# One block of a causal convolution as an unsplit fp32 product, in a kernel of long convolutions and a linear layer with adapters

## The chip, the cores and the metric

The kernel runs on one core of one Trainium2 chip. The metric is the device time of one execution in microseconds, the median over the runs. A core has five engines that work side by side and meet only through semaphores: TensorE (PE, matmuls; its weight loads are shown apart as PEld), VectorE (DVE), ScalarE (ACT), GpSimd (POOL) and SyncE (SP, which here only issues DMAs).

## What is computed

`x` is (128, 32, 512): 128 rows `b`, 32 heads `h`, 512 positions. Two residual steps follow each other.

```
# step 1: a causal convolution of every head with its own filter of 512 lags
A = -exp(log_A_real) + 1j*A_imag ;  dtA = A * exp(log_dt)          # 64 modes a head
K[h, l] = 2 * Re( sum_n C*(exp(dtA)-1)/A * exp(dtA * l) )          # l = 0..511
y[b,h,t] = sum_{s<=t} K[h,t-s] * x[b,h,s]  +  D[h]*x[b,h,t]        # reference: by FFT
x = x + where(t < length[b], y, 0)
# step 2: a linear layer 512 -> 512 with a rank-16 adapter chosen per row b
x = x + x @ W.T + bias + (x @ A[id[b]].T) @ B[id[b]].T
```

All is float32.

## The kernel before

**Numbers.** A float32 matmul here is made of three in the type fp32r: each operand is split into a rounded part (hi) and a remainder (lo), and hi*hi, hi*lo and lo*hi are added in PSUM. Only the small products that make the filters take float32 operands as they are (L904, L906).

**Filters.** The 512 lags of a filter are written as 16 coarse times 32 fine steps, so that the filter of a head is a product of a 128x16 and a 128x32 matrix (two halves of 64 modes). Heads are made in four groups of eight (`GROUPS`). Per group, VectorE makes the phases (`turns`, `phases`, `whole`, `fraction`), ScalarE the sines (`group_sines`, L469), VectorE the factors (`multiply`, `scale`, L703 to L710), with magnitudes from ScalarE's exponential (`mags`), and TensorE the products (`group`, L904, into `k_ps`). ScalarE rounds the result (L480, L483), VectorE makes the remainder (`k_low`, L667), and ScalarE issues the store of the hi and lo parts, beside each other, to a table `k_pad` in HBM (`group_store`, L488). The table has 128 zeros in front of each filter.

**Strips.** A convolution is a product with a Toeplitz matrix. It is made by a DMA that reads `k_pad` at 128 starts, one position apart, one for each partition: `strip[p, j] = K[j + p - 127]` with j = 0..511, hi and lo interleaved, 4 KB a partition, 512 KB a head (L256, SP's queue). There are `SS = 6` strip buffers: the load of head h waits until head h-6 is convolved.

**A head on TensorE** (`head`, L923). x lies as four blocks of 128 positions by 128 rows. For m = 0..3, the lags of block m are the weights (`strip[.., m*P:(m+1)*P, t]`, 128x128) and the first 4 - m blocks of x are moved, so 512, 384, 256 and 128 columns, each three times: 12 matmuls into one of four PSUM banks.

**Around it.** ScalarE rounds x of a head (`split_x`, L458), VectorE makes its remainder (L738) and, four heads later, multiplies the convolved head by the mask of lengths into `z_all` (L744). In the loop over heads these come in a fixed written order: mask of head h-4, remainder of head h, then a step of a later group (`STEPS_AT`). Four buffers hold a split head (`XS`), so a split waits for the head four before. Where TensorE makes a group between heads stands in `K_AFTER`: group 1 after head 0, group 2 after head 7, group 3 after head 14. Fifteen idle matmuls (`keep_warm`) run before head 0.

**SP's queue** issues, in written order and each behind its waits: parameters, x in pairs of heads (pairs 0 to 6 before the strips, pair 7 on ScalarE's queue, later ones between strips at `X_AT`), strips, adapter tables and weights (`A_AT`, `B_AT`, `W_AT`), the first x tiles. A DMA behind a waiting one waits too.

**Tiles.** Step 2 works on 32 tiles of 4 rows b x 32 heads. The first two tiles are begun when 30 heads are masked (`part_of_x1` L848, `part_of_remainder` L851, L575), the last two heads are added afterwards. Then TensorE runs per tile 4 matmuls of the adapters (L948), 12 of the weights (L960) and 2 of the gathered B rows (L986, L987).

Of the kernel before, what the change touches and what calls it, by code (L numbers as in the profile page):

```python
# [22 lines left out]
PAD = P + L  # L23
# [36 lines left out]
SS = 6  # L60
ZS = 4
# [11 lines left out]
PRE = 7  # L73
X_AT = {7: 8, 9: 9, 12: 10, 14: 11, 16: 12, 18: 13, 20: 14, 22: 15}
IDS_AT = 6
A_AT, B_AT, W_AT = {10: 0, 13: 1}, {15: 0, 17: 1}, {24: 0, 26: 1}
# [4 lines left out]
K_AFTER = {1: 0, 2: 7, 3: 14}  # L81
WARM = 15
# [6 lines left out]
def build(nc, x_conv, x_tile, params, table, d_row, length, ids_all, w_t, bias, a_t, b_rows, out):  # L89
    ctx = ExitStack()  # L90
    with ctx:
# [9 lines left out]
        k_pad = nc.dram_tensor("k_pad", (NH, PAD, 2), F32, kind="Internal").ap()  # L101
# [31 lines left out]
        k_sb = sb("k_sb", [NA, KS, G, NC, 2])  # L133
        d_sb = sb("d_sb", [1, NH])
        row0 = sb("row0", [1, NA])
        zero = sb("zero", [2 * NH, P])
# [4 lines left out]
        strip = sb("strip", [P, SS, L, 2], F32R)  # L141
# [17 lines left out]
        h_b = sb("h_b", [BR, TS, 2 * P])  # L159
        h_s = sb("h_s", [BR, TS, 2 * P])  # L160
# [12 lines left out]
        def y_bank(s):  # L173
# [8 lines left out]
        x_landed = [sem(f"x_landed{n}") for n in range(NH // XP)]  # L182
        strip_landed = [sem(f"strip_landed{s}") for s in range(SS)]
# [10 lines left out]
        scaled, exponents, mags, turn_ready, angle_ready, cs_ready, phased = (  # L194
            sem(n) for n in ("scaled", "exponents", "mags", "turn_ready", "angle_ready", "cs_ready", "phased"))
# [31 lines left out]
        def _(sp):  # L227
# [8 lines left out]
            def store_table(e, part, done):  # L236
# [8 lines left out]
            sp.wait_ge(zeroed, 1)  # L245
            sp.dma_start(k_pad[:, 0:P, :].rearrange("h (o p) e -> h o (p e)", o=2),
                         zero[0:NH, :].unsqueeze(1).to_broadcast((NH, 2, P))).then_inc(pad_stored, 16)
            sp.dma_start(len_sb[:, :], length).then_inc(len_in, 16)
# [74 lines left out]
        def _(pool):  # L323
# [9 lines left out]
            g.memset(zero[:, :], 0.0).then_inc(zeroed, 1)  # L333
# [113 lines left out]
        def _(act):  # L447
# [23 lines left out]
            def group_store(k):  # L471
# [14 lines left out]
                if k >= 1:  # L486
                    act.wait_ge(k_stored, 16 * k)
                act.dma_start(k_pad[h0:h1, P:PAD, :].rearrange("h (a c) e -> a h (c e)", a=NA),  # L488
                              k_sb[:, s, 0:n, :, :].rearrange("a h c e -> a h (c e)")
                              ).then_inc(k_stored, 16)  # L490

            act.wait_ge(par_in, 16)
# [4 lines left out]
            for h in range(GROUPS[0][1]):  # L497
                act.activation(mag[:, h, :], tab[:, 0:NL], ACT.Exp, scale=zr[:, h:h + 1]).then_inc(mags, 1)
# [3 lines left out]
            split_x(0)  # L502
            split_x(1)
            group_store(0)
            act.dma_start(z_all[:, PRE * XP:(PRE + 1) * XP, :, :].rearrange("p h c b -> p h (c b)"),
                          x_conv[:, PRE * XP:(PRE + 1) * XP, :]).then_inc(x_landed[PRE], 16)
            group_sines(1)
            magnitudes(GROUPS[1][0], NH, 1)
            split_x(2)
            split_x(3)  # L510
            for h in range(XS, NH):
# [89 lines left out]
        def _(dve):  # L601
# [61 lines left out]
            def k_low(k):  # L663
# [4 lines left out]
                                k_hi[:, 0:n, :].bitcast(F32), ALU.subtract).then_inc(k_lo_done, 1)  # L668

            def group(k):  # L670
# [36 lines left out]
                def scale():  # L707
                    dve.wait_ge(mags, GROUPS[0][1] + min(k, 1))
# [153 lines left out]
            for t in range(EARLY_T):  # L862
                dve.wait_ge(xhi_early, t + 1)
                part_of_remainder(t, 0, EARLY, xlo_early)
# [4 lines left out]
            for t in range(EARLY_T):  # L869
                dve.wait_ge(xhi_done, t + 1)  # L870
                part_of_remainder(t, EARLY, NH, xlo_done)
# [18 lines left out]
        def _(pe):  # L890
# [6 lines left out]
            def group(k):  # L897
# [3 lines left out]
                if k >= KS:  # L901
                    pe.wait_ge(k_lo_done, k + 1 - KS)
# [175 lines left out]
```

## Time and profile before

| | us |
|---|---|
| median of 3 runs | 214.99 (214.13 to 215.07) |
| the profiled execution | 215.08 |
| its span, first to last instruction | 212.1 |
| TensorE busy | 191.1 (90%) |
| VectorE busy | 167.8 (79%) |
| ScalarE busy | 115.3 (54%) |
| strip loads, issue to landing, median of 31 | 8.7 |
| granted TensorE clock | 1.00 |

A matmul record lasts longer than the matmul keeps the array, because successive ones overlap. What a matmul costs in a stream is therefore the distance from one to the next; the chain of waits gives it as a stretch of time over a count. A record shows a float32 shape for fp32r operands of matmuls too.

### The profile page before, as it was taken

The page shows a single profiled execution, that of the slowest core. Times are in us where ns is not written, and L with a number is a line of the kernel's source. Part 1 is how long each engine was busy: PE and PEld are TensorE (multiplying, and loading weights), DVE is VectorE, ACT ScalarE, POOL GpSimd, SP SyncE. Part 2 cuts the span into 40 slices and gives each one's busy share as a digit, 9 for nine tenths or more (in the row PEclk, how much of TensorE's full clock was granted, in tenths as well). Part 3 has the DMA queues.
Part 4 walks back from the last instruction along what each step waited for, and adds up shares of the span by engine and source line. Part 5 has one row for each costly group of instructions (what it writes and reads, how often), then busy time and mean ns, then how long its engine had stood idle before and what let it go on. Part 6 is the DMA issues. An engine that isn't in the chain of part 4 may idle for free.

```text
span 212.1 us, 4365 instructions
## 1 busy us (share of the span) xinstructions
PE 191.1 (90%) x1061; PEld 166.4 (78%) x1061; DVE 167.8 (79%) x367; ACT 115.3 (54%) x331; POOL 89.7 (42%) x144
## 2 busy tenths in 40 slices
PE   0048899999989999889999999999999999999994
PEld 0045699999979899878888888888888888888883
DVE  3988388799699677777998888878787888878662
ACT  2747146434545346328667565666657565666530
POOL 4750000000565739256646454544546464554600
PEclk9999999999999999999999999999999999999999
DMA  5956999999999999965677666777767776665334
GB/s 149 357 232 172 350 406 272 417 415 406 411 410 410 407 409 412 403 209 188 203 246 223 211 217 202 240 199 216 225 198 219 216 214 211 226 202 175 121 99 148
DMA packets 21520, 56.46 MB, mean 266 GB/s; under 512 B 3266, under 2 KB 3970, under 8 KB 21250
## 3 DMA queue, kind: packets, MB, share of 16 engines
q1 hardware_dynamic: 18226, 47.25, 62.1%
q0 software_dynamic: 2560, 8.39, 13.4%
q10 hardware_dynamic: 720, 0.66, 1.2%
q8 instruction: 5, 0.08, 0.1%
q14 instruction: 9, 0.07, 0.1%
HBM read 45.64 MB, written 10.65 MB: 265 GB/s over the span
## 4 chain that ended last, share of the span: by engine, by line
PE 80%; DMA 10%; DVE 6%; POOL 1%; issue 1%; ACT 0%; SPq 0%; DVEq 0%; ACTq 0%
PE z_ps L923 24%; PE y_ps L960 19%; PE k_ps L960 19%; DMA strip<-k_pad 8%; PE z_ps L948 7%; PE y_ps L987 2%; PE y_ps L986 2%; PE k_ps L987 2%; PE k_ps L986 2%; DMA par<-params 1%; DMA k_pad<-k_sb 1%; PE k_ps L904 1%; PE y_ps L1009 1%; PE k_ps L1009 1%; PE y_ps L970 1%
## 5 line engine op out<-in xcount | busy, mean ns | idle before, releaser
L923 PE MATMUL z_ps<-xp,strip 128*128 128x512 f32 (+3 forms) x384 | 64.4, 327 | 3.0 <-DMA strip<-k_pad 3.0
L923 PEld LDWEIGHTS z_ps<-xp,strip 128*128 128x128 f32 x384 | 59.4, 196 | 8.0 <-DMA strip<-k_pad 4.2
L413 POOL DMA_INDIRECT b_hl<-b_tab,b_idx x32 | 38.3, 1198 | 15.9 <-issue 9.8
L960 PE MATMUL y_ps<-w_hi,xp 128*128 128x512 f32 x120 | 39.5, 390 | 0.0
L408 POOL CAST ag<-a_hl 128x128 fp32r x64 | 21.9, 343 | 41.6 <-PE z_ps L948 30.3
L960 PE MATMUL k_ps<-w_hi,xp 128*128 128x512 f32 x120 | 39.5, 390 | 0.0
L539 ACT ACTIVATE ag<-a_hl 128x64 fp32r x128 | 25.8, 249 | 21.0 <-issue 20.7
L458 ACT ACTIVATE xp<-z_all 128x512 fp32r<-128x512 f32 x32 | 19.8, 629 | 23.4 <-PE z_ps L923 21.7
L744 DVE TENSOR_TENSOR z_all<-z_ps,mask 128x512 f32<-128x512 f32 (+2 forms) x33 | 22.2, 672 | 9.1 <-PE z_ps L923 8.6
L738 DVE TENSOR_TENSOR xp<-z_all,xp 128x512 fp32r<-128x512 f32 x32 | 24.3, 764 | 5.0 <-ACT xp L458 4.7
L960 PEld LDWEIGHTS y_ps<-w_hi,xp 128*128 128x128 f32 x120 | 22.6, 188 | 4.3
L960 PEld LDWEIGHTS k_ps<-w_hi,xp 128*128 128x128 f32 x120 | 22.6, 188 | 4.2
L559 ACT ACTIVATE h_hi<-h_m 64x128 fp32r<-64x128 f32 x64 | 19.5, 305 | 7.5 <-DVE h_m L803 5.5
L960 PE MATMUL y_ps<-w_lo,xp 128*128 128x512 f32 x60 | 23.4, 390 | 0.0
L960 PE MATMUL k_ps<-w_lo,xp 128*128 128x512 f32 x60 | 23.4, 390 | 0.0
L395 POOL TENSOR_TENSOR a_hl<-a_raw,a_hl 128x512 fp32r<-128x512 f32 x4 | 6.3, 1592 | 39.5 <-ACT a_hl L529 39.5
L948 PEld LDWEIGHTS z_ps<-xp,ag 128*128 128x128 f32 x128 | 19.4, 188 | 2.9
L793 DVE TENSOR_TENSOR xp<-x_t,xp 128x512 fp32r<-128x512 f32 x30 | 20.3, 677 | 0.7 <-ACT xp L547 0.7
L789 DVE TENSOR_TENSOR x_t<-x_t,z_all 128x512 f32<-128x512 f32 x30 | 20.4, 680 | 0.5 <-DMA x_t<-x_tile 0.5
L547 ACT ACTIVATE xp<-x_t 128x512 fp32r<-128x512 f32 x30 | 19.0, 632 | 2.7 <-DVE x_t L789 2.1
L948 PE MATMUL z_ps<-xp,ag 128*128 128x256 f32 x128 | 20.1, 280 | 0.0
L552 ACT ACTIVATE h_b<-z_ps 64x256 f32<-64x256 f32 x32 | 12.1, 379 | 13.4 <-PE z_ps L948 13.3
(139 smaller groups left out, 232.4 us busy)
## 6 DMA issues: line engine op xcount, KB each, us to landing
strip<-k_pad SPq DMA_DIRECT2D x31, 512.0 KB, 8.7
x_t<-x_tile SPq DMA_DIRECT2D x32, 256.0 KB, 2.7
out<-a_raw SPq DMA_DIRECT2D x31, 256.0 KB, 2.5
z_all<-x_conv SPq DMA_DIRECT2D x15, 512.0 KB, 8.5
a_raw<-a_t SPq DMA_DIRECT2D x2, 512.0 KB, 9.0
x_t<-b_rows SPq DMA_DIRECT2D x2, 512.0 KB, 10.7
w_sb<-w_t SPq DMA_DIRECT2D x2, 512.0 KB, 10.4
b_tab<-b_hl SPq DMA_DIRECT2D x1, 1024.0 KB, 10.1
```

The source lines that it names most:

```text
L408: last = g.tensor_copy(ag[:, s, :, :, q, :].rearrange("p c e r -> p e c r"), src)
L413: g.indirect_dma_start(out=b_hl[:, t % BS, :].bitcast(F32), out_offset=None, in_=b_tab, in_offset=bass.IndirectOffsetOnAxis(ap=b_idx[:, t: ...
L458: act.activation(xp[:, h % XS, :, 0, :], z_all[:, h, :, :], ACT.Copy).then_inc(xc_hi_done, 1)
L539: last = act.activation(ag[:, s, :, e, q, :], src[:, e, :, :], ACT.Copy)
L559: act.activation(h_hi[o:o + BR, b, :], h_m[:, b, :], ACT.Copy).then_inc(hhi_done, 1)
L738: V.tensor_tensor(xp[:, h % XS, :, 1, :], z_all[:, h, :, :], xp[:, h % XS, :, 0, :].bitcast(F32), ALU.subtract).then_inc(xc_lo_done, 1)
L744: V.tensor_tensor(z_all[:, h, :, b0:b1], in_chunks(z_ps[:, h % ZS, :])[:, :, b0:b1], mask[:, :, b0:b1], ALU.mult).then_inc(z_masked, 1)
L789: V.tensor_tensor(xt, xt, z_rows(t), ALU.add).then_inc(x1_done, 1)
L793: V.tensor_tensor(xp[:, s % XS, :, 1, :], in_chunks(x_t[:, s % XT, :]), xp[:, s % XS, :, 0, :].bitcast(F32), ALU.subtract).then_inc(xlo_do ...
L923: last = nc.tensor.matmul(z_ps[:, h % ZS, m * P:L], strip[:, h % SS, m * P:(m + 1) * P, t], xp[:, h % XS, 0:LC - m, e, :], start=(n == 0), ...
L948: last = nc.tensor.matmul(h_ps[:, s % TS, 0:2 * P], ag[:, s % TS, c, :, :, :].rearrange("p e b r -> p (e b r)"), xp[:, s % XS, c, :, :].re ...
L960: last = nc.tensor.matmul(y_bank(s), xp[:, s % XS, c, e, :], w[:, c, :], start=(n == 0), stop=False)
```

## The change

The block of the longest lags (m = 3, lags of 384 and more against the first 128 positions of x) is no longer three fp32r products. It is one product of unsplit float32 numbers: the lags from a new table `k_one` in HBM, without hi and lo, in which four heads are interleaved, and x as it was loaded. The strips keep 384 lags (3 KB a partition). A block `far` holds the far lags of four heads, 2 KB a partition, 256 KB a DMA, in three buffers. Each group therefore has two stores and each four heads one more load. The far weights of one head lie four words apart.

With it come moves in the written orders: group 1 is made ahead of head 0; its magnitudes, and the later ones, are single ScalarE activations placed between the splits in place of one VectorE product and one exponential over 24 heads; the padding and length DMAs go to ScalarE's queue and x pair 7 to SP's; some loads move by a head or so; and at the handover to the tiles VectorE makes the remainder of tile 1 after head 31's first mask instead of before it.

```
-PAD = P + L
+LM = L - P            # 384
+NQ = 4 ; ONE = 2 * P ; QS = 3
-PRE = 7
-X_AT = {7: 8, 9: 9, 12: 10, 14: 11, 16: 12, 18: 13, 20: 14, 22: 15}
-IDS_AT = 6 ; A_AT, B_AT, W_AT = {10: 0, 13: 1}, {15: 0, 17: 1}, {24: 0, 26: 1}
-SPLIT_B = {22: 0, 23: 1, 24: 2, 25: 3}
-K_AFTER = {1: 0, 2: 7, 3: 14} ; WARM = 15
+PRE = 8
+X_AT = {7: 8, 10: 9, 13: 10, 15: 11, 18: 12, 20: 13, 22: 14, 24: 15}
+IDS_AT = 5 ; A_AT, B_AT, W_AT = {9: 0, 12: 1}, {17: 0, 19: 1}, {24: 0, 26: 1}
+SPLIT_B = {23: 0, 24: 1, 25: 2, 26: 3}
+K_AFTER = {2: 7, 3: 14} ; WARM_0, WARM_1 = 15, 2
+MAGS_AT = {4: (24, 28), 5: (28, 32)}
...
# SP's queue
+            def load_last(q):
+                sp.wait_ge(last_stored, 16 * (q * NQ // G + 1))
+                src = bass.AP(tensor=k_one.tensor, offset=k_one.offset + NQ * (q * ONE + 1), ap=[[NQ, P], [1, P * NQ]])
+                sp.dma_start(far[:, q % QS, :, :].rearrange("p l x -> p (l x)"), src).then_inc(last_landed[q % QS], 16)
                 if h == 0:
                     load_strip(h, 0, 0, L // 2, strip_begun)
-                    load_strip(h, 0, L // 2, L, strip_landed[0])
+                    load_strip(h, 0, L // 2, LM, strip_landed[0])
+                    load_last(0)
                 else:
-                    load_strip(h, h % SS, 0, L, strip_landed[h % SS])
+                    if h > 0 and h % G == 0:
+                        load_last(h // NQ)
+                    load_strip(h, h % SS, 0, LM, strip_landed[h % SS])
+                if h % G == 2:
+                    load_last(h // NQ + 1)
...
# ScalarE: group_store, after the store to k_pad (group 0's copy is made by VectorE in k_low)
+                if k:
+                    act.wait_ge(last_stored, 16 * k)
+                    act.activation(k_last[...], k_ps[0:NA, s, 0:n * NC]..., ACT.Copy).then_inc(k_last_put, 1)
+                act.wait_ge(k_last_put, k + 1)
+                act.dma_start(k_one[h0 // NQ:h1 // NQ, :, :]..., k_last[NA // 2:NA, ...]).then_inc(last_stored, 16)
...
# ScalarE: order before the loop over heads
             group_sines(0)
             split_x(0)
+            magnitudes(*GROUPS[1])
+            group_store(0)
+            group_sines(1)
             split_x(1)
-            group_store(0)
-            act.dma_start(... x pair 7 ...)
-            group_sines(1)
-            magnitudes(GROUPS[1][0], NH, 1)
+            magnitudes(16, 18)
+            group_store(1)
             split_x(2)
+            magnitudes(18, 24)
             split_x(3)
...
# VectorE: start, and handover to the tiles
             fraction()
-            exponents_of(GROUPS[1][0], NH)
             remainder(0)
-            remainder(1)
             multiply()
             scale()
+            remainder(1)
+            k_low(1)
+            masks()
             remainder(2)
             remainder(3)
-            masks()
...
             part_of_x1(0, 0, EARLY, x1_early)
-            head(NH - 2)
             part_of_x1(1, 0, EARLY, x1_early)
-            both part_of_remainder(t, 0, EARLY, xlo_early)
+            head(NH - 2)
+            part_of_remainder(0, 0, EARLY, xlo_early)
             head(NH - 1, 0, EARLY_T * BT)
             part_of_x1(t, EARLY, NH, x1_done) for both tiles
-            part_of_remainder(t, EARLY, NH, xlo_done) for both tiles
+            part_of_remainder(0, EARLY, NH, xlo_done)
+            part_of_remainder(1, 0, EARLY, xlo_early)
+            part_of_remainder(1, EARLY, NH, xlo_done)
...
# TensorE
-                terms = [(m, t, e) for m in range(LC) for t, e in ((0, 0), (0, 1), (1, 0))]
+                terms = [(m, t, e) for m in range(LC - 1) for t, e in ((0, 0), (0, 1), (1, 0))]
                 ... the products of terms, as before ...
+                q = h // NQ
+                if h % NQ == 0:
+                    pe.wait_ge(last_landed[q % QS], 16 * (q // QS + 1))
+                nc.tensor.matmul(z_ps[:, h % ZS, LM:L], far[:, q % QS, :, h % NQ], z_all[:, h, 0, :],
+                                 start=False, stop=True).then_inc(conv_done, 1)
...
             group(0)
             pe.wait_ge(xc_hi_done, 1)
-            keep_warm(WARM)
+            keep_warm(WARM_0)
+            group(1)
+            keep_warm(WARM_1)
```

## Rows read from the trace of the kernel before

**Rows 1.** The page: busy time, share and count of TensorE.
```profile
PE 191.1 (90%) x1061; PEld 166.4 (78%) x1061; DVE 167.8 (79%) x367; ACT 115.3 (54%) x331; POOL 89.7 (42%) x144
```

**Rows 2.** The chain in order of time: start us, us, what.
```profile
25.33 13.85 PE z_ps L923 x84
39.17 0.57 PE k_ps L904 x16
...
60.48 11.17 DMA strip<-k_pad
71.70 15.90 PE z_ps L923 x96
87.62 0.69 DVE z_all L744
...
95.00 2.77 PE y_ps L960 x12
...
98.24 0.47 PE z_ps L948 x4
```

**Rows 3.** Timeline, VectorE, 80 to 84 us: start, busy, what [idle before].
```profile
81.74 0.69 DVE L744 TENSOR_TENSOR z_all<-z_ps,mask 128x512 f32<-128x512 f32 x1 [0.37 <-PE z_ps L923]
...
83.70 0.69 DVE L744 TENSOR_TENSOR z_all<-z_ps,mask 128x512 f32<-128x512 f32 x1 [0.19 <-PE z_ps L923]
```

**Rows 4.** Groups by form, TensorE: the unsplit products (busy, mean ns).
```profile
L904 PE MATMUL k_ps<-ee,gg 128*16 128x32 f32 x64 | 2.9, 205 | 13.5 <-DVE ee L710 13.5
```

**Rows 5.** Timeline, TensorE, around groups 1 and 3.
```profile
24.55 0.64 PE L904 MATMUL k_ps<-ee,gg 128*16 128x32 f32 x16
...
25.12 0.20 PE L906 MATMUL k_ps<-d_sb,row 1*16 1x8 f32 x2
...
25.26 5.06 PE L923 MATMUL z_ps<-xp,strip 128*128 128x512 f32 x28
...
53.84 0.46 PE L904 MATMUL k_ps<-ee,gg 128*16 128x32 f32 x10
```

**Rows 6.** Groups by form, weight loads: strided strip, contiguous x, 16 columns.
```profile
L923 PEld LDWEIGHTS z_ps<-xp,strip 128*128 128x128 f32 x384 | 59.4, 196 | 8.0 <-DMA strip<-k_pad 4.2
L960 PEld LDWEIGHTS k_ps<-w_hi,xp 128*128 128x128 f32 x120 | 22.6, 188 | 4.2
...
L904 PEld LDWEIGHTS k_ps<-ee,gg 128*16 128x16 f32 x64 | 2.4, 104 | 13.7 <-issue 13.4
```

**Rows 7.** Stretches: engines' busy time, granted clock, DMA share, GB/s at the end.
```profile
50.00:60.00 10.00, 10.00 (x76) 9.32 (x75) 8.30 (x15) 5.84 (x11) 4.60 (x4) 1.00 1.03 409
```

**Rows 8.** DMA issues: the stores of filters, KB each, us to landing.
```profile
k_pad<-k_sb ACTq DMA_DIRECT2D x4, 32.0 KB, 5.5
```

**Rows 9.** The strip loads' line (L256), all of them.
```profile
DMA to landing us min/median/max: 4.0/8.5/11.6
```

**Rows 10.** Waits: engine, line, for whom, us in total, times, longest.
```profile
PE z_ps L923 <- DMA strip<-k_pad: 3.0, 5, 1.3
...
SPq L256 <- DMA k_pad<-k_sb: 3.3, 2, 2.3
```

**Rows 11.** Timeline of the start, 6 to 38 us, ScalarE and VectorE.
```profile
6.44 1.89 ACT L498 ACTIVATE mag<-tab,zr 128x48 f32<-128x48 f32 x8
...
14.67 0.37 ACT L480 ACTIVATE k_hi<-k_ps 16x256 fp32r<-16x256 f32 x1 [2.72 <-PE k_ps L906]
...
17.27 1.28 ACT L463 ACT_TABLE_LOAD   x1
...
27.35 0.69 DVE L738 TENSOR_TENSOR xp<-z_all,xp 128x512 fp32r<-128x512 f32 x1 [1.17 <-ACT xp L458]
...
37.84 0.42 DVE L710 TENSOR_TENSOR ee<-work,mag 128x256 f32<-128x256 f32 x1
```

**Rows 12.** Timeline of the handover to the tiles, VectorE.
```profile
88.79 1.41 DVE L851 TENSOR_TENSOR xp<-x_t,xp 128x480 fp32r<-128x480 f32 x2
...
90.12 0.18 DVE L744 TENSOR_TENSOR z_all<-z_ps,mask 128x32 f32<-128x32 f32 x1
```

More of the change, by code:

```diff
@@ L22 @@
 BR = BT * R
-PAD = P + L
+LM = L - P
+NQ = 4
+ONE = 2 * P
 assert NA * NC == L and 2 * NS == P and 2 * BR == P
@@ L60 @@
 SS = 6
+QS = 3
 ZS = 4
@@ L99, in sem @@
             return ctx.enter_context(nc.semaphore(name))
-        k_pad = nc.dram_tensor("k_pad", (NH, PAD, 2), F32, kind="Internal").ap()
+        k_pad = nc.dram_tensor("k_pad", (NH, P + LM, 2), F32, kind="Internal").ap()
+        k_one = nc.dram_tensor("k_one", (NH // NQ, ONE, NQ), F32, kind="Internal").ap()
         b_tab = nc.dram_tensor("b_tab", (2 * AD * R, L), F32, kind="Internal").ap()
@@ L140, in build @@
         pos = mask[:, :, :].bitcast(I32)
-        strip = sb("strip", [P, SS, L, 2], F32R)
+        strip = sb("strip", [P, SS, LM, 2], F32R)
+        far = sb("far", [P, QS, P, NQ])
         xp = sb("xp", [P, XS, LC, 2, P], F32R)
@@ L159, in build @@
         h_b = sb("h_b", [BR, TS, 2 * P])
+        zero = h_b[:, 0, 0:P]
         h_s = sb("h_s", [BR, TS, 2 * P])
@@ L182, in build @@
         x_landed = [sem(f"x_landed{n}") for n in range(NH // XP)]
+        last_landed = [sem(f"last_landed{s}") for s in range(QS)]
+        last_stored, k_last_put = sem("last_stored"), sem("k_last_put")
         strip_landed = [sem(f"strip_landed{s}") for s in range(SS)]
@@ L193, in build @@
             sem(n) for n in ("ea_ready", "zr_ready", "th_ready", "rc_ready", "rec_ready", "ez_ready"))
-        scaled, exponents, mags, turn_ready, angle_ready, cs_ready, phased = (
-            sem(n) for n in ("scaled", "exponents", "mags", "turn_ready", "angle_ready", "cs_ready", "phased"))
+        scaled, mags, turn_ready, angle_ready, cs_ready, phased = (
+            sem(n) for n in ("scaled", "mags", "turn_ready", "angle_ready", "cs_ready", "phased"))
         k_hi_put = sem("k_hi_put")
@@ L496, in _, with magnitudes @@
             act.wait_ge(table_in, 16)
-            for h in range(GROUPS[0][1]):
-                act.activation(mag[:, h, :], tab[:, 0:NL], ACT.Exp, scale=zr[:, h:h + 1]).then_inc(mags, 1)
+            def magnitudes(h0, h1):
+                for h in range(h0, h1):
+                    act.activation(mag[:, h, :], tab[:, 0:NL], ACT.Exp, scale=zr[:, h:h + 1]).then_inc(mags, 1)
+            magnitudes(*GROUPS[0])
             act.wait_ge(angle_ready, 1)
@@ L519, in _ @@
                         group_sines(k)
+                if h in MAGS_AT:
+                    magnitudes(*MAGS_AT[h])
                 if h in SPLIT_B:
@@ L858, in _ @@
             part_of_x1(0, 0, EARLY, x1_early)
-            head(NH - 2)
             dve.wait_ge(xt_landed[1], 16)
             part_of_x1(1, 0, EARLY, x1_early)
-            for t in range(EARLY_T):
-                dve.wait_ge(xhi_early, t + 1)
-                part_of_remainder(t, 0, EARLY, xlo_early)
+            head(NH - 2)
+            dve.wait_ge(xhi_early, 1)
+            part_of_remainder(0, 0, EARLY, xlo_early)
             head(NH - 1, 0, EARLY_T * BT)
@@ L868, in _ @@
                 part_of_x1(t, EARLY, NH, x1_done)
-            for t in range(EARLY_T):
-                dve.wait_ge(xhi_done, t + 1)
-                part_of_remainder(t, EARLY, NH, xlo_done)
+            dve.wait_ge(xhi_done, 1)
+            part_of_remainder(0, EARLY, NH, xlo_done)
+            dve.wait_ge(xhi_early, 2)
+            part_of_remainder(1, 0, EARLY, xlo_early)
+            dve.wait_ge(xhi_done, 2)
+            part_of_remainder(1, EARLY, NH, xlo_done)
             head(NH - 1, EARLY_T * BT, NB)
@@ L902, in group @@
                     pe.wait_ge(k_lo_done, k + 1 - KS)
+                    pe.wait_ge(k_last_put, k + 1 - KS)
                 for i in range(h1 - h0):
@@ L922, in head @@
                         pe.wait_ge(strip_landed[0], 16)
-                    last = nc.tensor.matmul(z_ps[:, h % ZS, m * P:L], strip[:, h % SS, m * P:(m + 1) * P, t],
-                                            xp[:, h % XS, 0:LC - m, e, :], start=(n == 0), stop=(n == len(terms) - 1))
-                last.then_inc(conv_done, 1)
+                    nc.tensor.matmul(z_ps[:, h % ZS, m * P:L], strip[:, h % SS, m * P:(m + 1) * P, t],
+                                     xp[:, h % XS, 0:LC - m, e, :], start=(n == 0), stop=False)
+                q = h // NQ
[3 more added lines that the diff above has]
+                                 start=False, stop=True).then_inc(conv_done, 1)
             pe.wait_ge(d_in, 16)
```

46 lines of the change are left out of this document (23 added, 23 removed).

## The prediction

> **What bounds the kernel now.** I read the page first: TensorE is busy 90% of the span [rows 1]. Then the chain in order of time [rows 2]. It has three parts: a start until about 25 us (parameters, filter of the first eight heads, stored and read back as strips), 32 convolution heads until 87.62 + 1.96 = 89.6, and 32 tiles to the end. In the tiles the chain never leaves TensorE, and the change touches nothing there: that part stays.
>
> In the convolution part the chain is almost all TensorE: 84 matmuls (7 heads) in 13.85 us, and one step of 11.17 us on the strip loads, from 60.48 on. Undisturbed, a head takes 83.70 - 81.74 = 1.96 us [rows 3]. Beside it the DMA engines are full (share 1.03, 409 GB/s) [rows 7]. TensorE stood 3.0 us for strips in 5 waits, 1.3 for the very first [rows 10]. What the later ones cost is read from the chain: head 15 begins at 39.88 + 13.85 + 0.71 = 54.4, head 23 at 71.70, 17.3 us for 8 heads that need 15.7: 1.6 lost. So two resources lie close together here. A cheaper head is worth its full price only where the strips keep up.
>
> **A head.** Removed: three matmuls of 128 columns. Added: one product of unsplit fp32, 128 x 128 x 128. Prices of the nine that stay: 512 columns 2.77 / 12 = 0.23 us, 256 columns 0.47 / 4 = 0.118 [rows 2], 384 columns between them, 0.174. 3 x (0.23 + 0.174 + 0.118) = 1.57. The three narrow ones and the uncovered first weight load of the next head therefore cost 1.96 - 1.57 = 0.39.
>
> The fp32 product is not in the trace at this size. L904 is the nearest: 64 matmul records for 32 products [rows 4], so an unsplit product is two loads and two matmuls. Ten of them end 0.46 us after the first begins, and one lasts 0.19 or 0.20 (mean 205 ns, the slower first group included): (0.46 - 0.19) / 9 = 0.030 us apart for 32 columns [rows 5]. Four times the columns give 4 x 0.030 = 0.12 each, 0.24 for the two, and a matmul of 0.12 covers the next load of 128 columns about exactly (a 256-column one does so at 0.118). Bounds: below, each pass at half of that, 0.12 for the pair and some 0.06 of load left uncovered; above, either of the first two rivals. I take 0.24, and 0.02 to 0.03 because the strip's loads are slower than L960's (196 against 188 ns [rows 6]): 1.57 + 0.24 + 0.02 = 1.83. **A head saves 0.13 us.**
>
> The rate is the same as four passes of 128 columns at 2.4 GHz, 0.21 us. The Trainium skill (FP8 and Floating Point Precision, TensorE Precision Notes) says that true fp32 takes four passes; by it alone the pair is 0.21 and the head 1.80. The trace's 0.24 stands in the sum.
>
> **The start.** Group 1's 18 matmuls (25.26 - 24.55 = 0.71 us [rows 5]) move from behind head 0 to ahead of it. Their cover there is the wait for the first strip. Group 1's factors come about as early as before: the deferred exponents (1.3 us of VectorE) are gone, but ScalarE now issues a second store and loads the sine table (1.28, as the exponential one [rows 11]) before the sines. The eight magnitudes of group 1 (1.89 us for eight) and their table fit, to a few tenths, into ScalarE's wait of 2.72 us before the first k_hi and the split that moves away from there [rows 11]. Ahead of strip 1's end the queue holds 256 + 128 KB of strip 0, 256 KB of the far block and 384 KB: 1024 KB as now (256 + 256 + 512). It gains only what pair 7, moved from ScalarE's queue to the front, took away, 512 KB or 1.28 us at most; I take 0.9. Head 1 starts at about 24.4 instead of 25.26, and group 1 is no longer between. Moving the padding and lengths to ScalarE's queue costs 0.8 us there, before parameters at 2.9 us that it waits for anyway: nothing.
>
> This gain does not all reach head 8. In heads 4 to 9 VectorE runs nearly without a gap: remainder 4 begins at 27.35, after ScalarE [rows 11], and group 2's scaling ends at 37.84 + 0.42 = 38.26. After the change ScalarE has 16 single magnitudes (0.24 each) and a further table load among splits 2 to 5, so remainder 4 starts no earlier (I get 27.2), and the factors of group 2 are again there at 38.25. TensorE would end head 7 at 24.4 + 7 x 1.83 = 37.2 and waits 1.0 us. Head 8 then starts at 39.0 instead of 39.88 (39.17 and 0.71 of group 2 [rows 2]): **-0.8**. If ScalarE were not late, it would be up to -1.8.
>
> **Heads 8 to 31.** 7 heads, group 3 as now, 17 heads: 24 x 0.13 = **-3.1**, as long as strips land.
>
> **The strips.** A head loads 384 KB, and 64 KB as its share of a far block, instead of 512 KB: at 409 GB/s 1.12 us instead of 1.28, 12.5% less, where the head on TensorE gets 7% shorter. Against it stands SP's queue, which now waits for two stores of a group, the second about 0.9 us behind the first on ScalarE's queue (copy 0.45, issue 0.36); a store lands 5.5 us after its issue [rows 8], and SP waits for it already now (3.3 us in 2 waits [rows 10]). What is queued behind that wait is every later strip and x pair, six heads ahead of TensorE. For head 16: group 2 done at 39.0, its three copies behind masks and splits 2.1, the second store 0.9 more, 5.5 to land: 47.5, with the queue then nearly run dry, and the first landing 4.0 later at the least [rows 9]. From 51.5 to strip 25 stand 10 strips (0.96), 3 far blocks (0.64) and 7 other loads (1.28), 20.5 us, the first of them landed: 71.4, where TensorE wants head 25 at 39.0 + 7 x 1.83 + 0.8 + 10 x 1.83 = 70.9. So half a microsecond is lost there and some at heads 19 to 21; bounds 0 and 2.7 more than now. I leave the present 1.6: **0**.
>
> **The handover to the tiles.** Now head 31's mask, due at 89.6, waits for two remainders (88.79 to 90.2) and runs at 90.12 [rows 12]. The change puts only one before it: **-0.5**. The second is 0.7 us and is due only for tile 1, some 3.5 us after the first matmul. The table stores and x_tile loads follow the strips by the same order and come earlier with them.
>
> **Sum:** -0.8 - 3.1 - 0.5 = -4.4. The profiled execution took 215.08 (span 212.1 and 3.0 around it), the median is 214.99: 215.1 - 4.4 = **210.7**.
>
> **Rivals.**
>
> *A break at each change of number type (0.18).* The pipeline empties where the matmul's kind changes. [Rows 5] show it: 16 matmuls 0.030 apart should take 0.48, but L906 begins 0.57 after the first, 0.09 late, and the convolution's first is also late by 0.08; then the next load of 128 columns (0.11) is uncovered. These changes are of shape, one of them without a change of type, which speaks against; all changes of type are also changes of shape, so nothing excludes it. The change makes two per head: 2 x (0.09 + 0.11) = 0.40, a head of 2.23, +0.27 x 31 = 8.4. The strips then are never late (-1.6), the start gives -0.9, the handover -0.5: +5.4, **220.5**. It decides once the two breaks cost more than 0.13 a head.
>
> *Weights four words apart (0.12).* The far block has four heads interleaved, so its weights are read at every 16th byte. Two words apart already costs 196 against 188 ns [rows 6]. If a load takes double, 0.236, it is no longer covered: 0.236 + 0.236 + 0.12 after eight matmuls of 1.47 is 2.07, +0.11 x 31 = 3.4, less the same 3.0: **215.5**, no change. The Trainium skill (SBUF — State Buffer, Door 1: The DMA port swizzle) says that reads need two hits in each 16-byte line for full bandwidth, which the strip has and the far block has not, though the same passage calls a stride of 4 fp32 free. No row here reads weights so.
>
> *The queue (0.10).* The mechanism is right but the second store and the far blocks make SP late at heads 8, 16 and 24, and the engines restart slowly after running dry. The strips then give back 2.7: **213.3**.
>
> **Chances.** My forecast has 0.60, with a range of its own of 208.6 to 212.5 (the DMA waits gone and half a microsecond elsewhere, or 1.8 more waits); with the queue 0.10, the strided load 0.12, the break 0.18. The range for all is 208.6 to 216.2, which leaves out the break. Half a percent, 1.1 us, is what a measurement here can tell from none: faster holds the first case and most of the queue, 0.67; same, the rest and half of the strided load, 0.13; slower 0.20.
>
> **What would show it.** The masks of late heads 1.83 us apart; two loads and two matmuls of about 0.12 for the far block, the next head's load close behind; a wait of TensorE for the scaling of group 2 of about 1 us; head 8 at 39.0; the last head done near 85.5; head 31's first mask right after it. Wrong would be: masks 2.07 or 2.2 apart, gaps around the far matmuls, TensorE standing for far blocks, or a table load that delays split 2 and with it head 2.

## The result, and the profile after

The changed kernel takes **213.34 us** (median of 4 runs, 213.16 to 213.79), the kernel before 215.00 (4 runs): a ratio of 0.9935, 95% interval 0.9906 to 0.9965. It is faster by 0.7%, where 210.7 us (2.0%) was forecast. The profiled executions differ by 215.08 - 213.79 = 1.29 us, and only 0.4 of that is span (212.1 to 211.7). The rest is time around the span, 3.0 and 2.1 us. The profiled execution of the kernel after is the slowest of its four; the others have spans of 211.1 to 211.3.

The page of the kernel after, its engines line (it answers to [rows 1]):

```profile
PE 193.8 (92%) x1031; PEld 169.6 (80%) x1031; DVE 167.6 (79%) x367; ACT 123.0 (58%) x359; POOL 90.3 (43%) x144
```

Thirty matmuls fewer (1061 to 1031), and yet TensorE is busy 2.7 us longer. The groups by form say which instruction is dear (busy us, mean ns of one | idle before). First the matmuls of the convolution, then weight loads; L955 is the strip (L923 before), L960 the far block, L998 the tiles (L960 before), L936 the unsplit products of the filters:

```profile
L955 PE MATMUL z_ps<-xp,strip 128*128 128x512 f32 x96 | 30.2, 422 | 0.3 <-DMA strip<-k_pad 0.3
...
L960 PE MATMUL z_ps<-z_all,far 128*128 128x128 f32 x64 | 20.0, 394 | 0.3 <-DMA far<-k_one 0.3
```
```profile
L955 PEld LDWEIGHTS z_ps<-xp,strip 128*128 128x128 f32 x288 | 49.7, 197 | 4.1 <-DMA strip<-k_pad 0.5
L998 PEld LDWEIGHTS k_ps<-w_hi,xp 128*128 128x128 f32 x120 | 22.5, 188 | 4.2
...
L960 PEld LDWEIGHTS z_ps<-z_all,far 128*128 128x128 f32 x64 | 17.5, 322 | 0.5 <-DMA far<-k_one 0.5
```

64 records for 32 products: an unsplit product is two loads and two matmuls here too. A load of the far block lasts 322 ns, against 197 for one whose weights are two words apart and 188 for words side by side [rows 6]. The waits for strips have gone from 3.0 us to 0.3. The timeline of three heads in the middle, matmuls and then loads (start, busy, what; the last row of each is cut by the end of the window), answers to [rows 3]:

```profile
67.04 1.83 PE L955 MATMUL z_ps<-xp,strip 128*128 128x512 f32 x9
68.70 0.62 PE L960 MATMUL z_ps<-z_all,far 128*128 128x128 f32 x2
69.08 1.83 PE L955 MATMUL z_ps<-xp,strip 128*128 128x512 f32 x9
70.74 0.62 PE L960 MATMUL z_ps<-z_all,far 128*128 128x128 f32 x2
71.12 1.12 PE L955 MATMUL z_ps<-xp,strip 128*128 128x512 f32 x4
```
```profile
68.58 0.55 PEld L960 LDWEIGHTS z_ps<-z_all,far 128*128 128x128 f32 x2
69.03 1.02 PEld L955 LDWEIGHTS z_ps<-xp,strip 128*128 128x128 f32 x5
```

A head is 69.08 - 67.04 = 2.04 us, where 1.83 was forecast and 1.96 was there before. Two far loads take from 68.58 to 69.03, when the next head's load begins: 0.45 us for two, with matmuls of 0.12 to cover them. That is where the gain of the head went, as e1 to e4 and e7 show below.

The start and the handover, TensorE and VectorE (they answer to [rows 5] and [rows 12]):

```profile
24.40 1.85 PE L955 MATMUL z_ps<-xp,strip 128*128 128x512 f32 x9 [0.27 <-DMA strip<-k_pad]
...
87.44 1.83 PE L955 MATMUL z_ps<-xp,strip 128*128 128x512 f32 x9
...
90.69 1.17 PE L1008 MATMUL y_ps<-w_hi,xp 128*128 128x512 f32 x4 [0.97 <-ACT xp L606]
```
```profile
88.33 0.65 DVE L880 TENSOR_TENSOR xp<-x_t,xp 128x480 fp32r<-128x480 f32 x1
89.76 0.19 DVE L773 TENSOR_TENSOR z_all<-z_ps,mask 128x32 f32<-128x32 f32 x1 [0.78 <-PE z_ps L960]
```

| start on TensorE, us | before | after | difference |
|---|---|---|---|
| head 1 | 25.26 | 24.40 | -0.86 |
| head 8 | 39.81 | 39.59 | -0.22 |
| head 15 | 54.35 | 54.76 | +0.41 |
| head 23 | 71.70 | 71.12 | -0.58 |
| head 31 | 87.42 | 87.44 | +0.02 |
| first tile | 91.05 | 90.69 | -0.36 |

The account of the profiled executions closes. Head 1 gains 0.86. Seven heads at +0.08 and 23 more at +0.08 give back 2.4. The 1.6 us of waits for late strips, read from the chain as lost between heads 15 and 23, are gone. The handover gives 0.37. Together -0.4, the difference of the spans.

### The profile page after: what moved, and what is told of

It is laid out like the page before. It is cut to its first block, busy times and chain, and to the rows that moved or that the text cites. A ratio compares the mean times of both kernels' runs of the same rounds, so it can differ in the third digit from the quotient of the medians.

```text
span 211.7 us, 4345 instructions
## 1 busy us (share of the span) xinstructions
PE 193.8 (92%) x1031; PEld 169.6 (80%) x1031; DVE 167.6 (79%) x367; ACT 123.0 (58%) x359; POOL 90.3 (43%) x144
## 4 chain that ended last, share of the span: by engine, by line
PE 87%; DVE 5%; DMA 4%; POOL 1%; issue 1%; SPq 1%; ACT 0%; DVEq 0%; ACTq 0%
PE z_ps L955 23%; PE y_ps L998 19%; PE k_ps L998 19%; PE z_ps L986 7%; PE z_ps L960 7%; DMA strip<-k_pad 3%; PE y_ps L1025 2%; PE y_ps L1024 2%; PE k_ps L1025 2%; PE k_ps L1024 2%; DMA par<-params 1%; DMA k_pad<-k_sb 1%; PE y_ps L1047 1%; PE k_ps L1047 1%; PE y_ps L1008 1%
## 5 line engine op out<-in xcount | busy, mean ns | idle before, releaser
L955 PE MATMUL z_ps<-xp,strip 128*128 128x512 f32 (+2 forms) x288 | 58.4, 347 | 0.3 <-DMA strip<-k_pad 0.3
L955 PEld LDWEIGHTS z_ps<-xp,strip 128*128 128x128 f32 x288 | 49.7, 197 | 4.1 <-DMA strip<-k_pad 0.5
L424 POOL CAST ag<-a_hl 128x128 fp32r x64 | 23.3, 368 | 43.1 <-PE z_ps L986 29.5
L998 PE MATMUL k_ps<-w_hi,xp 128*128 128x512 f32 x120 | 39.5, 390 | 0.0
L998 PE MATMUL y_ps<-w_hi,xp 128*128 128x512 f32 x120 | 39.5, 390 | 0.0
L767 DVE TENSOR_TENSOR xp<-z_all,xp 128x512 fp32r<-128x512 f32 x32 | 25.8, 807 | 8.2 <-ACT xp L474 8.1
L998 PEld LDWEIGHTS k_ps<-w_hi,xp 128*128 128x128 f32 x120 | 22.5, 188 | 4.2
L998 PEld LDWEIGHTS y_ps<-w_hi,xp 128*128 128x128 f32 x120 | 22.5, 188 | 4.2
L998 PE MATMUL y_ps<-w_lo,xp 128*128 128x512 f32 x60 | 23.4, 390 | 0.0
L998 PE MATMUL k_ps<-w_lo,xp 128*128 128x512 f32 x60 | 23.4, 390 | 0.0
L960 PE MATMUL z_ps<-z_all,far 128*128 128x128 f32 x64 | 20.0, 394 | 0.3 <-DMA far<-k_one 0.3
```

What stands on the lines that cost most here:

```text
L424: last = g.tensor_copy(ag[:, s, :, :, q, :].rearrange("p c e r -> p e c r"), src)
L767: V.tensor_tensor(xp[:, h % XS, :, 1, :], z_all[:, h, :, :], xp[:, h % XS, :, 0, :].bitcast(F32), ALU.subtract).then_inc(xc_lo_done, 1)
L955: nc.tensor.matmul(z_ps[:, h % ZS, m * P:L], strip[:, h % SS, m * P:(m + 1) * P, t], xp[:, h % XS, 0:LC - m, e, :], start=(n == 0), stop=F ...
L960: nc.tensor.matmul(z_ps[:, h % ZS, LM:L], far[:, q % QS, :, h % NQ], z_all[:, h, 0, :], start=False, stop=True).then_inc(conv_done, 1)
L998: last = nc.tensor.matmul(y_bank(s), xp[:, s % XS, c, e, :], w[:, c, :], start=(n == 0), stop=False)
```

## The experiments

All are variants of the changed kernel, except e8, which is the kernel before with one order altered; e5, e6, e9 and e10 alter two or more things, as said at each. "Head" is the distance of two heads' first matmuls where nothing waits. Times are medians, and the span is that of the profiled execution. The kernel before ran beside each group and took 213.88 us in one group and 214.96 in another, so runs of different groups are compared by their ratios, not by their times.

| run | us | before beside it | ratio, 95% interval | span | far load, ns | head, us |
|---|---|---|---|---|---|---|
| after | 213.34 | 215.00 | 0.9935 (0.9906 to 0.9965) | 211.7 | 322 | 2.04 |
| e1_contig | 211.23 | 214.96 | 0.9835 (0.9757 to 0.9913) | 208.6 | 191 | 1.79, 1.83 |
| e2_pairs | 212.70 (one) | 214.96 | | 210.6 | 196 | 1.80, 1.83 |
| e3_rounded4 | 212.22 (one) | 214.96 | | 210.1 | 313 | 1.81 |
| e4_rounded1 | 214.18 (one) | 214.96 | | 212.1 | 192 | 1.70 |
| e5_contig_ids | 211.48 | 213.88 | 0.9876 (0.9835 to 0.9917) | 208.9 | | |
| e6_pairs_ids | 210.83 | 213.88 | 0.9837 (0.9794 to 0.9880) | 209.0 | 196 | 1.80, 1.83 |
| e7_strides | 212.12 (one) | 213.88 | | 210.0 | 186 to 330 | 1.79 to 2.04 |
| e8_handover | 213.71 (one) | 213.88 | | 211.6 | | |
| e9_spread | 211.58 | 214.91 | 0.9858 (0.9824 to 0.9891) | 209.3 | 196 | 1.80, 1.83 |
| e10_spread_order | 211.85 | 214.91 | 0.9864 (0.9833 to 0.9894) | 209.8 | 196 | 1.80, 1.83 |

**e1_contig: the same product, its weights side by side.** The far block is stored and loaded head by head instead of four heads interleaved; the same bytes, in rows of 512 B instead of 2 KB, and the same number of DMAs and matmuls. The source address of the load and the copies before the stores follow the new order and are left out here.

```diff
+IL = 1
+IN = NQ // IL
-k_one = nc.dram_tensor("k_one", (NH // NQ, ONE, NQ), ...)
+k_one = nc.dram_tensor("k_one", (NH // IL, ONE, IL), ...)
-far = sb("far", [P, QS, P, NQ])
+far = sb("far", [P, QS, IN, P, IL])
...
-nc.tensor.matmul(z_ps[...], far[:, q % QS, :, h % NQ], z_all[:, h, 0, :],
+nc.tensor.matmul(z_ps[...], far[:, q % QS, h % NQ // IL, :, h % IL], z_all[:, h, 0, :],
```

> The changed kernel with the far lags of each head by themselves (in the table k_one, in the stores and in the block far), so that the far weights are read contiguously; the bytes are the same, in rows of 512 B instead of 2 KB. Theory 1, the stride: a load at every 16th byte takes twice as long, so here the two far loads last about 190 ns in the profile instead of 322, the head goes from 2.04 to 1.83 us and the waits that I predicted appear (group 2's factors, about 1 us, and some strips): 210.5 to 212. Theory 2, the number type: a load of 128 columns of unsplit fp32 takes 0.22 us however it lies: loads 322 ns, heads 2.04, 213.3. Theory 3, a break at each change of type: also 2.04 and 213.3, with loads that start late.

**e2_pairs: weights two words apart**, as the strip's are (`IL = 2`).

> The changed kernel with the far lags of two heads interleaved instead of four: weights two words apart, as in the strips. Theory 1 with a 16-byte line as the limit: as with contiguous weights, loads near 196 ns and heads of 1.83 us, total within 0.5 us of that run. Theory 1 with a cost that grows with the stride: loads near 250 ns, heads of 1.9. Theories 2 and 3: 2.04 and 213.3.

Far loads of e1 and e2, and the timeline of a late head of e1:

```profile
L963 PEld LDWEIGHTS z_ps<-z_all,far x64: 187/191/192, 23.1 to 86.2; 128*128 128x128 f32 x64
```
```profile
L963 PEld LDWEIGHTS z_ps<-z_all,far x64: 194/196/331, 23.0 to 88.2; 128*128 128x128 f32 x64
```
```profile
78.99 1.86 PE L958 MATMUL z_ps<-xp,strip 128*128 128x512 f32 x9
80.68 0.39 PE L963 MATMUL z_ps<-z_all,far 128*128 128x128 f32 x2
80.82 1.86 PE L958 MATMUL z_ps<-xp,strip 128*128 128x512 f32 x9
```

With side-by-side weights the load is 191 ns and the head 80.82 - 78.99 = 1.83 us (1.79 in heads 1 to 7), where 1.83 was forecast. So the pair of unsplit fp32 matmuls was priced about right, the break at each change of number type that the first rival charged with 0.40 us a head is not there (it would have stayed), and the whole 0.21 us by which the head missed is the distance of the weights. Two words apart (e2) are as good as one. The time fell to 211.23, by 2.1 us, not by 31 x 0.21 = 6.5: the first tile starts 3.15 us earlier than in the kernel after (87.54). What eats the other 3.4 is the second question. e2 had e1's head and only 212.70, in one execution.

**e3_rounded4 and e4_rounded1: is it the number type?** The far product is one rounded (fp32r) product of x's high part instead of the unsplit one; the low part's share is left out. Weights four words apart in e3 and side by side in e4:

```diff
-far = sb("far", [P, QS, P, NQ])
+far = sb("far", [P, QS, IN, P, IL], F32R)          # IL = 4 in e3, 1 in e4
-... z_all[:, h, 0, :],
+... xp[:, h % XS, 0, 0, :],
```

> The changed kernel with the far block taken as fp32r and multiplied with the rounded part of x alone: one load and one matmul instead of two and two (it leaves out the remainder of x and part of the lags' precision in the far block). The weights lie four words apart as in the change. Theory 1: this load lasts about 322 ns too, though its type is fp32r, and the head is about 1.90 us (1.47 for eight matmuls, 0.12, 0.22 for the load, 0.12 for the next head's). Theory 2 and 3: the load lasts 197 ns and the head takes 1.57 + 0.06 + 0.06 + 0.06 = 1.75.

> The same single fp32r product with the far weights contiguous (it leaves out the same parts). Theories 1, 2 and 3 all expect a load of 188 ns and a head of about 1.75 us on TensorE, where strips allow it; beside the run with four words it shows what the stride alone costs in type fp32r. The time is then set by the strips: 209 to 211.

Far loads of e3, then e4:

```profile
L963 PEld LDWEIGHTS z_ps<-xp,far x32: 309/313/313, 22.9 to 87.7; 128*128 128x128 f32 x32
```
```profile
L963 PEld LDWEIGHTS z_ps<-xp,far x32: 186/192/331, 23.1 to 88.4; 128*128 128x128 f32 x32
```

The load costs the same 313 ns in fp32r: the price is that of the distance, not of the number type. A single dear load costs the head 1.81 - 1.70 = 0.11 us, a pair 0.24 (2.04 - 1.80): each load beyond its cover by about 0.12. And e4, with one product in fp32r, has a head 0.10 us below e2's with a pair in unsplit fp32: one more matmul of 128 columns and nothing for a change of type.

e4 missed its 209 to 211 us. The shortest head of all, 1.70, has the longest span of the variants, 212.1. Its waits are longer, and two of its heads run at half the clock. Stretches of e4 (engines' busy time, granted clock, DMA share, GB/s), and its timeline there:

```profile
60.00:64.00 4.00, 3.74 (x22) 3.21 (x20) 3.90 (x6) 2.19 (x4) 3.48 (x3) 1.00 1.05 414
64.00:68.00 4.00, 0.84 (x2) 0.78 (x3) 3.93 (x7) 1.15 (x2) 1.83 (x2) 0.79 1.05 377
68.00:72.00 4.00, 4.00 (x14) 3.52 (x14) 3.94 (x7) 1.15 (x2) 0.19 (x1) 0.50 1.02 399
```
```profile
67.16 3.22 PE L958 MATMUL z_ps<-xp,strip 128*128 128x512 f32 x9 [3.24 <-DVE xp L770]
...
70.28 3.10 PE L958 MATMUL z_ps<-xp,strip 128*128 128x512 f32 x9
```

TensorE stood 3.24 us for VectorE and then ran two heads at 0.50 of the clock, 1.2 GHz, 3.1 and 3.0 us instead of 1.70. e2 stood 3.24 us as well and ran one head slowly, 3.3 us. In e1 the wait at this place was 1.74, and the clock stayed at 1.00. But e3 stood longest, 3.28 us at the same place, and its clock stayed at 1.00 too (its timeline and its stretch of the wait):

```profile
68.01 1.83 PE L958 MATMUL z_ps<-xp,strip 128*128 128x512 f32 x9 [3.28 <-DVE xp L770]
```
```profile
64.00:68.00 4.00, 0.73 (x6) 0.61 (x5) 3.90 (x7) 1.31 (x3) 2.58 (x2) 1.00 1.04 401
```

So a wait of this length does not by itself bring the slow stretch, and what decides stays open. The slow head is 1.5 us of the 2.0 by which the profiled executions of e1 (210.67) and e2 (212.70) differ. Each variant has one profiled execution; one of e1's four runs, 212.72 us at a mean clock of 0.992, resembles e2, and two runs of the kernel before beside them, 217.06 and 215.95 us, show a mean clock of 0.984.

**What the wait is.** VectorE of e1 (start, busy, what), then its TensorE:

```profile
60.94 1.32 DVE L751 CAST id_f<-ids 128x160 f32<-128x160 int32 x1
62.30 0.25 DVE L752 TENSOR_SCALAR id_f<-id_f 128x160 f32<-128x160 f32 x1
...
63.50 1.17 DVE L757 TENSOR_SCALAR b_idx<-ids,tab 128x32 int32<-128x32 int32 x1
...
66.38 1.17 DVE L770 TENSOR_TENSOR xp<-z_all,xp 128x512 fp32r<-128x512 f32 x1
```
```profile
65.96 1.82 PE L958 MATMUL z_ps<-xp,strip 128*128 128x512 f32 x9 [1.74 <-DVE xp L770]
```

In step 20 of its loop VectorE computes the adapter numbers for the tiles, which select each row's adapter, in six instructions, from 60.94 to 64.67. A head leaves VectorE 0.46 us beside its mask and remainder (1.83 - 0.69 - 0.68), so it is late for head 21, by 2.0 us with the restart. The kernel after does the same work (61.83 to 64.6) and TensorE does not wait: there a head leaves 0.67 us and VectorE has more lead.

**e5_contig_ids and e6_pairs_ids: the six instructions in step 16 instead of 20**, with the far weights of e1 (`IL = 1`) and of e2 (`IL = 2`).

```diff
-                if h == 20:
+                if h == 16:
                     adapter_ids()
```

> Contiguous far weights, and the adapter ids (six VectorE instructions) made in the loop's step 16 instead of 20. In the run with contiguous weights TensorE stood about 2 us before head 21, where VectorE was busy with the ids from 60.9 to 64.7, two of them at 1.2 to 1.3 us instead of 0.25 while GpSimd worked. Theory A (VectorE late with remainder 21): the wait goes, about 1 us of strip waits takes its place (strip 21 landed at 65.34, where head 21 would start at 64.3), 209.3 to 210.5. Theory B (the strips are the limit in any case): no gain, 211.2.

> The same with the far lags of two heads interleaved (rows of 1 KB instead of 512 B; the loads had measured the same 196 ns). Theory A: the 3.5 us wait before head 21 and the stretch at half clock behind it both go, 209 to 210; if the larger rows help the strips, up to 0.5 us below the contiguous one. Theory B: 212.5.

The wait is gone from head 21 and stands elsewhere. ScalarE of e6, and the strips' waits of e6 (engine, what <- releaser: us in total, times, longest):

```profile
57.26 0.30 ACTq L502 DMA_DIRECT2D k_pad<-k_sb  x1
57.60 0.40 ACT L507 ACTIVATE k_last<-k_ps 16x256 f32<-16x256 f32 x1 [4.13 <-DVE k_sb L695]
...
58.40 0.63 ACT L477 ACTIVATE xp<-z_all 128x512 fp32r<-128x512 f32 x1 [0.40 <-PE z_ps L963]
```
```profile
PE z_ps L958 <- DMA strip<-k_pad: 1.2, 2, 0.9
```

Group 3's low half is now late on VectorE (56.78), ScalarE waits for it 4.13 us with the splits of two heads queued behind, head 18 starts 1.7 us late, and the strips of heads 25 and 27, behind group 3's stores, are late by 1.2 in all. It is the queue behind a waiting instruction that the prediction feared, for another reason. Both theories missed: e6 forecast 209 to 210 and e5 209.3 to 210.5, against 210.83 and 211.48. e6 has the lowest time of all, but before beside it was low as well: its ratio, 0.9837, is e1's 0.9835. That the move gained anything over e1 is not shown. Over e2 it is likely, as the wait of 3.24 us and the slow head are gone.

**e7_strides: distances of one to four words in one kernel.** The far weights of heads 0 to 7, 8 to 15, 16 to 23 and 24 to 31 are read 1, 2, 3 and 4 words apart; except for heads 0 and 4 the words read are not the head's own, so its far product is another. How the block is stored and loaded is the same for all heads.

```diff
+... far[...].rearrange("p i l x -> p (i l x)")[:, 0:(h // 8 + 1) * (P - 1) + 1:h // 8 + 1], ...
```

> The kernel with contiguous far lags, whose far weights are read with steps of 1 (heads 0 to 7), 2 (8 to 15), 3 (16 to 23) and 4 words (24 to 31) (for the steps over 1 these are other lags than the reference's: the far product is left wrong there, the work is the same). Theory 1 as a limit of a 16-byte line with two reads in it: steps 1 and 2 load in 190 to 197 ns, step 3 in between (128 reads over 96 lines, 1.33 to a line), some 260, step 4 322. Theory 1 as a cost that starts only at a full line: steps 1 to 3 all at 190 to 200.

Two loads per head; rows of a head with one, two, three and four words:

```profile
29.15 0.30 PEld L963 LDWEIGHTS z_ps<-z_all,far 128*128 128x128 f32 x2
```
```profile
50.56 0.32 PEld L963 LDWEIGHTS z_ps<-z_all,far 128*128 128x128 f32 x2
```
```profile
67.27 0.43 PEld L963 LDWEIGHTS z_ps<-z_all,far 128*128 128x128 f32 x2
```
```profile
83.24 0.55 PEld L963 LDWEIGHTS z_ps<-z_all,far 128*128 128x128 f32 x2
```

Single loads: 186 to 191, 194 to 196, 256 or 261, 312 or 330 ns; heads 1.79 to 1.83, 1.80 to 1.83, 1.92 to 1.94, 2.04. As the block arrives in the same rows in all four stretches, the distance alone makes the difference. From two words on the price rises by about 0.06 us a word: 128 weights cover 64, 96 and 128 pieces of 16 bytes at two, three and four words, and the load follows that count. From 32 pieces (one word) to 64 it rises by 5 ns only. The distance itself fits these points as well as the count of pieces; more than four words, which would tell the two apart, were not run.

**e8_handover: the kernel before with the new order of the handover alone.**

```diff
-            for t in range(EARLY_T):
-                dve.wait_ge(xhi_early, t + 1)
-                part_of_remainder(t, 0, EARLY, xlo_early)
+            dve.wait_ge(xhi_early, 1)
+            part_of_remainder(0, 0, EARLY, xlo_early)
...
+            dve.wait_ge(xhi_early, 2)
+            part_of_remainder(1, 0, EARLY, xlo_early)
```

> The kernel before with only the handover's new order on VectorE (the remainder of tile 1 after head 31's first mask). From the start of head 31's first matmul to the first tile's first one it took 3.63 us before and 3.26 in the changed kernel, whose head is 0.08 longer. I expect 3.15 to 3.2 here, a gain of 0.45, and the span at 211.6 instead of 212.1. The rival is that the gain needs the longer head: then 3.6.

```profile
89.64 0.19 DVE L744 TENSOR_TENSOR z_all<-z_ps,mask 128x32 f32<-128x32 f32 x1 [0.70 <-PE z_ps L925]
```

From the start of head 31 to the first tile it is 3.10 us (87.47 to 90.57) against 3.63 before: the 0.5 is there, in one execution. In the time it isn't shown: 213.71 us and a span of 211.6 stand beside seven executions of the kernel before with a median of 213.88 and spans of 211.4 to 212.8.

**e9_spread and e10_spread_order: the same work in small pieces, one in each of steps 19 to 23**, with weights two words apart (`IL = 2`). The pieces of `adapter_ids` are its instructions in order, the last two together.

```diff
-                if h == 20:
-                    adapter_ids()
+                if h in IDS_STEPS:            # {19: 0, 20: 1, 21: 2, 22: 3, 23: 4}
+                    adapter_ids(IDS_STEPS[h])
...                                            # e10 alone:
-X_AT = {..., 24: 15}    W_AT = {24: 0, 26: 1}
+X_AT = {..., 23: 15}    W_AT = {25: 0, 27: 1}
```

> The changed kernel with the far block interleaved by pairs of heads (weights two words apart), and adapter_ids cut into five pieces that VectorE does at heads 19, 20, 21, 22 and 23, after the low half of group 3's filters, instead of all of it at one head. Theory (what is left of the gain is lost where VectorE is late by 2 to 4 us at one head, and not on TensorE): a piece costs VectorE 0.3 to 1.3 us, one head's slack each; the stalls of 1.7 us at heads 17 and 20 both shrink below 0.7, group 3's stores leave as in the kernel before, head 1.80 to 1.83, time 209.3 to 210.2. Rival (the strips' queue is the limit: a head spared in one place is waited for in the next): stalls move to heads 18 to 25 as waits for strips, 210.6 to 211.2, as with the ids at head 16 in one piece (210.83).

> As e9_spread, and on the load queue the last x pair one head earlier (step 23 instead of 24, ahead of the wait for group 3's second store) and the two halves of the weight w each one step later (25 and 27 instead of 24 and 26). Theory (strip 24 and 25 are late because 512 KB of w and the x pair are issued between the last far block and them): strips 24 and 25 land 0.6 to 1.3 us earlier, the waits at heads 24 and 25 fall by as much, 0.3 to 1 us less than e9_spread. Rival (what the queue spends is the same sum wherever it stands, or those waits are not there any more): within 0.2 us of e9_spread, or later tiles pay for w.

VectorE of e9, its five steps:

```profile
60.01 1.33 DVE L753 CAST id_f<-ids 128x160 f32<-128x160 int32 x1
...
62.96 0.23 DVE L755 TENSOR_SCALAR id_f<-id_f 128x160 f32<-128x160 f32 x1
...
64.43 1.42 DVE L757 TENSOR_TENSOR id_f<-id_f 128x160 f32<-128x160 f32 x1
...
67.09 1.34 DVE L759 TENSOR_SCALAR id_f<-id_f 128x160 f32<-128x160 f32 x1
...
70.08 0.23 DVE L761 CAST ids<-id_f 128x160 int32<-128x160 f32 x1
```

Theory missed, and the rival's number (210.6 to 211.2) too: 211.58 and 211.85. The same cast is 0.23 us in step 16 of e6 and 1.33 here; the six instructions are 1.52 us busy in e6, 3.56 in e1 and 4.8 in e9. GpSimd of e1 shows why:

```profile
57.49 4.67 POOL L414 TENSOR_TENSOR a_hl<-a_raw,a_hl 128x512 fp32r<-128x512 f32 x3 [5.13 <-ACT a_hl L563]
63.35 1.27 POOL L420 TENSOR_TENSOR a_raw<-x_t,b_hl 128x512 f32<-128x512 f32 x1 [1.19 <-ACT b_hl L558]
```

Its three operations end at 62.16, VectorE's cast of 60.94 at 62.26; its fourth ends at 64.62, VectorE's b_idx of 63.50 at 64.67, both shown further up. These instructions, begun beside such an operation of GpSimd, end with it or shortly after. The remainders that begin there last 1.17 to 1.20 us instead of 0.68. The masks, which read PSUM, are not held; this one of e1 lies within the 4.67 us:

```profile
59.25 0.68 DVE L776 TENSOR_TENSOR z_all<-z_ps,mask 128x512 f32<-128x512 f32 x1
```

Five pieces over five heads meet three of these operations, where one block met two. So the pieces cost more than they spread, and the waits moved to heads 20, 22, 23 and 24 (0.8, 0.5, 1.2 and 0.5 us). e9 also stood 1.17 us for the factors of group 3 at 52.5 us, ahead of all pieces, where e1, e6 and e10 did not stand; why is open. e10 says nothing for or against the queue's order: the late strips 24 and 25 that it was to mend are not there in e9 (0.2 us of waits on strips, at head 1) nor in e10 (0.5, at head 1).

## Why the prediction was wrong, and where it was right

The step that failed is in "A head": "a matmul of 0.12 covers the next load of 128 columns about exactly". That is so for weights up to two words apart. The far block has them four apart, the two loads take 0.45 us, about 0.225 each, and nothing covers 0.11 of each. The measured 213.34 lies above the forecast's own range (208.6 to 212.5). It is nearly the number of the rival "the queue", 213.3, whose mechanism is not there: strips and far blocks were waited for 0.6 us in all, so that agreement is luck. The sizes:

- **The head**, 1.83 forecast, 2.04 measured. The term -3.1 for heads 8 to 31 was +1.8 to head 31. With the distance taken away (e1, e2) the head is 1.79 to 1.83: the pair's 0.24 and the nine strip matmuls' 1.57 were right to a few hundredths together. The rival "weights four words apart" had the mechanism and the head (2.07), with a chance of 0.12; its 215.5 was 1.7 us above the profiled execution, since it charged 0.11 a head where the head grew by 0.08 (0.9 in 31 heads), and the time around the span fell by 0.9.
- The rule of the Trainium skill (SBUF — State Buffer, Door 1: The DMA port swizzle) on two hits in each 16-byte line fits what was measured here, and the sentence beside it that calls a stride of 4 fp32 free does not. The strip has two hits (196 ns), the far block one (322 ns), and e7 shows the price between them (258 ns at three words).
- **The start**: head 1 at 24.4 forecast, 24.40 measured; the variants, with the same start, have it between 23.53 and 24.13, so the hundredth is luck. Of the -0.8 up to head 8 only -0.22 was left, since seven longer heads came between.
- **The wait for group 2's factors** did not come, because head 7 itself ended later. Where the head is short it is there: 0.62 us in e1, head 8 at 38.26, where 1.0 and 39.0 were forecast. In e1 the factors came 0.7 earlier than I had them (scaling done at 37.51). The other variants with such a head have it between 0.26 (e5) and 1.24 us (e2), so it was right in kind and its size differs from run to run.
- **The strips**: 1.6 us of waits were left at 1.6; they are 0.3 in all after, since a head of 2.04 asks for less than the queue brings. With the short head they are back (e1: 0.24, 0.32 and 0.43 us at heads 18, 19 and 20). For a group's second store SP waited once in the kernel after, 1.5 us, and no strip was late by it; in e1 it waited three times for it, 8.7 us in all, so with the short head the queue that the prediction feared is in part there.
- **The handover**: -0.5 forecast, -0.4 in the kernel after, whose head 31 is 0.08 longer, and -0.5 alone (e8).
- **The break at each change of type** does not exist: load and matmul of the far block follow the strip's as any others (e1's head leaves no room for it).
- **The time around the span** was taken as fixed at 3.0. In seven runs of before beside e5, e6 and e8 it lay between 2.05 and 2.98, in after at 2.1 each time. So up to 0.9 of the measured 1.7 is not the change's work in the span; that the change caused any of it isn't shown.

What would have followed with the head right: the sum said 210.7, e6 measures 210.83 and e1 211.23. That agreement is partly luck. Against the kernel before beside them e6 is 3.05 us and e1 3.7 us faster, where the sum had 4.4. e1's first tile is 3.5 us earlier than before's, where the sum had 4.4. The sum left out VectorE's step 20, 2.0 us at head 21; the start, group 2 and the strips came out 0.3, 0.4 and 0.4 cheaper. VectorE's slack of a head falls from 0.59 to 0.46 us with a head of 1.83; I priced VectorE in heads 4 to 9 only.

Open: whether a kernel with neither wait reaches 208 or 209, since no place was found for the adapter numbers that costs nothing; what the time around the span depends on; and why the clock fell after the wait in e2 and e4 and not in e3.

## What to carry to other kernels

Before an operand's layout is changed so that one DMA serves several heads, look at how TensorE reads it: here a load of 128 weights cost 0.13 us more with its words four apart than with two, and the short matmul beside it, 0.12 us, could not hide that. When a stage's step is made shorter, go through every engine's once-only work in that stage (here six instructions of VectorE in one step) and hold it against the new slack, at the speed that this engine has there with the others at work. And compare spans as well as times when a gain of half a percent is in question.

## What the hardware showed that I had not expected

- A load of 128 x 128 weights takes 188 to 191, 196, 258 and 322 ns with its words 1, 2, 3 and 4 apart, the same in fp32r (313) as in fp32.
- The same VectorE cast of 128 x 160 numbers took 0.23 us with GpSimd idle (e6) and 1.32 or 1.33 beside a tensor operation of GpSimd (e1, e9), ending with it. The Trainium skill (SBUF — State Buffer, Who interferes with whom) says that the two share a pair of ports as an exclusive lock; these rows agree. The masks, which take one input from PSUM, kept their 0.68 us.
- After TensorE had stood 3.24 us for VectorE, one head (e2) or two (e4) ran at 1.2 GHz, 3.0 to 3.3 us each; after 1.74 us (e1) and also after 3.28 us (e3) the granted clock stayed at 1.00. A long wait can so cost twice, but did not each time, and with it a kernel with a shorter head can end later.
